# Edges sorted in two halves, the second while the first is written, then added; lists sorted by levels within the rounds

## The reference

```python
# 1: gated graph layer, five rounds on h = layernorm(x)
m = h @ weight[i]
agg = segment_sum(m[src] * edge_attr[:, None], dst)
h = gru_cell(agg, h, w_ih, w_hh, b_ih, b_hh)
# 2: gelu layer with 8 experts, one chosen per node
# 3: graph attention with 8 heads over the same src, dst (sums by src)
# 4: 16 experts, two chosen per node, layernorm
```

## Time and profile before

| | us |
|---|---|
| median of three runs (lowest, highest) | 6021.33 (6021.12, 6024.78) |
| the profiled execution | 6021.4 |
| its span in the trace | 6020.1 |
| PE busy in the span | 4223.5 |
| DVE busy | 2594.2 |
| POOL busy | 2375.9 |
| ACT busy | 1810.6 |

### The profile page before, as it was taken

The page is one execution under the profiler, slowest core; times in us unless marked ns, Lnnn a source line. Parts: engine busy times, 40 slices in busy tenths (PEclk is TensorE's granted clock), DMA queues, the critical chain, the costliest instruction groups (busy, mean ns, idle before and its releaser), DMA issues. The chain is left out here.

```text
span 6020.1 us, 61157 instructions
## 1 busy us (share of the span) xinstructions
PE 4223.5 (70%) x17097; PEld 2593.1 (43%) x17097; DVE 2594.2 (43%) x5613; ACT 1810.6 (30%) x3960; POOL 2375.9 (39%) x2850
## 2 busy tenths in 40 slices
PE   1111113457999999999997859477787767996693
PEld 0110101223544545545444337366666654554372
DVE  8887760112222222122124113655555567776235
ACT  4551000000000101001001311466666648995121
POOL 3336777777000000000000022577777756884303
PEclk9998556778999999999999878799989988997697
DMA  9001001121332231322231323488778855776223
GB/s 397 7 0 46 1 3 44 44 88 44 109 108 98 97 109 65 125 95 86 105 114 43 112 77 117 130 244 242 235 242 242 242 179 171 237 237 226 68 65 111
DMA packets 366136, 752.69 MB, mean 125 GB/s; under 512 B 81332, under 2 KB 186328, under 8 KB 346105
## 3 DMA queue, kind: packets, MB, share of 16 engines
q1 hardware_dynamic: 234825, 575.73, 27.5%
q0 software_dynamic: 77328, 145.78, 9.4%
q10 hardware_dynamic: 53664, 27.26, 1.6%
HBM read 538.83 MB, written 209.74 MB: 124 GB/s over the span
## 5 line engine op out<-in xcount | busy, mean ns | idle before, releaser
L929 PE MATMUL PS<-mem 128*128 128x512 f32 (+1 forms) x3500 | 1363.6, 551 | 318.5 <-DMA mem<-adjacency 314.6
L929 PEld LDWEIGHTS PS<-mem 128*128 128x128 f32 x3500 | 629.5, 192 | 1035.8 <-issue 718.8
L1698 POOL DMA_INDIRECT mem<-gat_rows,mem x832 | 810.4, 974 | 258.2 <-issue 230.0
L522 POOL DMA_INDIRECT adjacency<-mem x782 | 777.3, 994 | 284.1 <-issue 253.4
L1034 DVE COPY mem<-PS 128x512 f32<-128x512 f32 (+1 forms) x35 | 21.8, 624 | 1631.3 <-PE PS L929 1631.3
L1073 POOL MEMSET mem<- 128x256 f32 x1 | 0.3, 311 | 1773.1 <-ACT mem L980 1773.1
L250 PE MATMUL PS<-mem 112*128 112x112 f32 (+3 forms) x462 | 106.5, 410 | 625.6 <-DVE mem L363 272.7
L993 ACT ACTIVATE mem<-PS 128x512 f32<-128x512 f32 (+1 forms) x35 | 19.0, 543 | 1615.6 <-PE PS L929 1615.6
L2042 PE MATMUL PS<-mem 128*128 128x264 f32 x1660 | 451.5, 410 | 29.5 <-DVE mem L2002 19.6
L1733 PE MATMUL PS<-mem 128*128 128x128 f32 x1664 | 280.3, 295 | 248.6 <-DMA mem<-gat_rows,mem 247.9
L1779 ACT ACTIVATE mem<-PS,mem 128x256 f32<-128x256 f32 x832 | 424.4, 561 | 13.7
(11 more groups left out here) (386 smaller groups left out, 6766.0 us busy)
## 6 DMA issues: line engine op xcount, KB each, us to landing
mem<-adjacency SPq DMA_DIRECT2D x150, 1280.0 KB, 5.4
gathered_rows<-mem SPq DMA_DIRECT2D x416, 264.0 KB
mem<-gathered_rows SPq DMA_DIRECT2D x208, 528.0 KB, 4.4
adjacency<-mem SPq DMA_DIRECT2D x56, 800.0 KB, 20.7
mem<-edge_slots ACTq DMA_DIRECT2D x26, 1024.0 KB, 8.3
mem<-w SPq DMA_DIRECT2D x32, 512.0 KB
mem<-gat_rows,mem POOLq DMA_INDIRECT x832
hidden_rows<-mem SPq DMA_DIRECT2D x25, 512.0 KB, 3.0
```

The source lines that it names most:

```text
L522: g.indirect_dma_start(AD[:, :], bass.IndirectOffsetOnAxis(ap=aidx[:, k:k + 1], axis=0), SF[:, k:k + 1], None).then_inc(s[f"scattered{n % ...
L929: ins = t.matmul(PS[:, f, 0:n], lhsT=h[:, b, f * 128:(f + 1) * 128], rhs=m.pan[i % NPAN][:, j, 0:n], start=(b == 0), stop=(b == NB - 1))
L1698: g.indirect_dma_start(m.Dg[i % RING][:, k, j, :], None, HD[:, :], bass.IndirectOffsetOnAxis(ap=L.idxD[:, c:c + 1], axis=0)).then_inc(s[f" ...
```

## The change

The edges are taken in two halves of 50,000, in the order in which they come (so the second has no smaller `dst` than the first). Each half is sorted on 98x512 values (four turns' worth of 128 columns instead of seven; 392 values on the N side) with 136 steps and 18 turns, and has its own key, weight, sum and address buffers. The first half goes as before. Its 391 scatters then run on POOL while DVE, ACT and PE sort the second half; since POOL is taken, DVE makes the masks of the second half itself, with a third compare per step. When all scatters of the first half have landed, POOL issues those of the second with `compute_op=ALU.add`, so that a cell which both halves hold gets both sums; the region behind the matrix is zeroed too. The counts for the panels are those of the second half.

The list sort is cut into levels. The first steps and levels 1 to 3 come before the rounds; levels 4 to 10 and the last part come one each after an iteration q of the rounds, levels 4 to 8 in the first round at q = 0 to 4, the rest in the second at q = 0 to 2. Each level has a turn at the start of PE's next q and one after the third panel of its gather, both in one PSUM bank, so that the second four transposes wait until DVE has read the first four. For this the turned h uses one bank instead of two. There are three panel buffers instead of four, loads for lists and rounds are issued right after the zeroing instead of after the edge sort, and the lists are stored behind the last panel.

```diff
-T1 = 784
+HALF = E // 2
+ROWS1 = 98
+T1 = 4 * ROWS1
...
+    if second:
+        masks, _ = like(m.D[n % NK], old)
+        if n >= NK:
+            v.wait_ge(*s["swapped"](n - NK + 1))
+        for (a, b), k in zip(old, masks):
+            ins = v.tensor_tensor(k, a, b, ALU.is_gt)
+        ins.then_inc(s["mask"].sem, 1)
...
-NCELL = (E + 127) // 128
+NCELL = (HALF + 127) // 128
 CGRP = 8
...
+            g.wait_ge(*sc[f"{name}{n % 2}"](16 * CGRP * (n // 2)))
+        at = bass.IndirectOffsetOnAxis(ap=aidx[:, k:k + 1], axis=0)
+        if add:
+            g.indirect_dma_start(AD[:, :], at, SF[:, k:k + 1], None,
+                                 compute_op=ALU.add).then_inc(sc[f"{name}{n % 2}"].sem, 16)
+        else:
+            g.indirect_dma_start(AD[:, :], at, SF[:, k:k + 1], None).then_inc(sc[f"{name}{n % 2}"].sem, 16)
...
+def listed_at(l, q):
+
+    if q < 5:
+        level = EARLY + 1 + 5 * l + q
+        return level if level <= LAST_LEVEL + 1 else None
...
+def lists_turn(t, m, s, PS, ident, turn, banks):
+
+    level, back = turn // 2 + 1, turn % 2
+    i, n, _ = steps_until(level)
+    if back:
+        i, n = i + level + 1, n + level
+    t.wait_ge(*s["keys"](n))
+    parts = list(turn_parts(m, "toT" if back else "toN", m.K[i % 2], 0))
+    for h in range(2):
+        t.wait_ge(*s["turned"](1 + 2 * turn + (h if banks[0] == banks[1] else 0)))
+        for src, (_, rows, cols) in parts[4 * h:4 * h + 4]:
+            ins = into(t, PS, (src, (banks[h], rows, cols)), ident)
+        ins.then_inc(s["kt"].sem, 1)
...
-NPAN = 4
+NPAN = 3
...
         for q in range(NG + 1):
+            level = listed_at(l, q - 1) if q else None
+            if level:
+                lists_turn(t, lm, li, PS, ident, 2 * level - 2, BANKS)
             if q < NG:
-                rounds_gather(t, m, s, PS, l, q)
+                rounds_gather(t, m, s, PS, l, q, ident, lm, li, level)
...
+        if k == 2 and level and level <= LAST_LEVEL:
+            lists_turn(t, lm, li, PS, ident, 2 * level - 1, BANKS)
...
-    t.wait_ge(*s["ht"](NB + i - 1))
+    t.wait_ge(*s["ht"](NB + i))
...
+            level = listed_at(l, q)
+            if level and level <= LAST_LEVEL:
+                lists_level(v, lm, cn, li, PS, level, BANKS)
+            elif level:
+                lists_last(v, lm, L, li, lst, PS, BANKS)
```

More of the change, by code:

```diff
@@ L154, in network @@
             yield "T", "plain", 1 << i
-    for level in range(1, 11):
+    for level in range(1, levels + 1):
         yield "toN", level, 0
@@ L373, in edges_swap @@
     new, _ = halves(m.W[where][1 - buf][0:P], C, kind, block)
-    masks, mask = like(PS[:, 4 + n % NMASK, :].bitcast(I32), old)
+    masks, mask = like((m.D[n % NK] if second else PS[:, 4 + n % NMASK, :]).bitcast(I32), old)
     v.wait_ge(*s["mask"](n + 1))
@@ L405, in edges_vector @@
                 v.wait_ge(*hd["table"](16))
-            edges_order(v, m, cn, s, PS, plan, i)
+            edges_order(v, m, cn, s, PS, plan, i, second)
         if i >= 2 and plan[i - 2][0] in "TN":
-            edges_swap(v, m, s, PS, *plan[i - 2])
-CELLS = "step edges_ps nb_rows nb_ps local tails_ps carry carry_ps sums back sf cells scattered0 scattered1 held held_ps due"
-def cells_memory(ar, ed, cn):
-    m = Box()
[L419 to L424, removed]
-    return m
+            edges_swap(v, m, s, PS, second, *plan[i - 2])
@@ new lines, with cells_memory @@
+CELLS = {"edges_ps": 1, "nb_rows": 2, "nb_ps": 1, "local": 2, "tails_ps": 1, "carry": 1, "carry_ps": 1, "sums": 2, "back": 1,
+         "sf": 1, "cells": 1}
+SCATTER = "step first0 first1 scattered0 scattered1 held held_ps due"
+def cells_memory(ar):
+    m = Box()
+    m.EQ, m.SX = ar.mk(513)[0:ROWS1], ar.mk(512)[0:ROWS1]
+    m.rows = ar.mk(6, ROWS1)
+    m.cinc, m.aone = ar.mk(1)[0:ROWS1], ar.mk(1)[0:ROWS1]
+    m.ki, m.ia, m.ib = (ar.mk(512, dt=I32)[0:ROWS1] for _ in range(3))
+    m.fa = ar.mk(512)[0:ROWS1]
+    return m
@@ L627, in lists_tensor, with lists_first @@
              stop=True).then_inc(s["counts_ps"].sem, 1)
[L628 to L648 removed]
+    for turn in range(2 * EARLY):
+        lists_turn(t, m, s, PS, cn.ident, turn, EARLY_BANKS)
+def lists_first(v, m, cn, s, st, PS):
     A, K = m.A, m.K
@@ new lines, in lists_level0, with lists_level @@
+def lists_level0(v, m, s):
+    i = 0
+    for k in range(1, 8):
+        for e in range(k, 0, -1):
+            lists_compare(v, m, s, i, i, 0, "T", "flip" if e == k else "plain", 1 << e)
+            i += 1
+def lists_level(v, m, cn, s, PS, level, banks):
+    i, n, turn = steps_until(level)
+    for where, steps in (("toN", level), ("toT", 7)):
+        for h in range(2):
+            v.wait_ge(*s["kt"](2 * turn + h + 1))
+            turn_keys(v, m, cn, PS, where, level, m.K[(i + 1) % 2], banks[h], h).then_inc(s["turned"].sem, 1)
+        i, turn = i + 1, turn + 1
+        for e in range(steps, 0, -1):
+            kind = "flip" if where == "toN" and e == level else "plain"
+            lists_compare(v, m, s, i, n, 2 * turn, where[2], kind, 1 << e)
+            i, n = i + 1, n + 1
```

447 lines of the change are left out of this document (235 added, 212 removed).

## The result

The changed kernel takes 6153.5 us (median of 4 runs, 6152.67 to 6155.08), the kernel before beside it 6023.06 (6021.12 to 6028.02): **1.0216 times as long, 95% interval 1.0198 to 1.0233**. I had forecast 5929 us. The profiled execution took 6153.57 us with a span of 6152.3, 132.2 us more than the span of before.

A forecast was written before the change was run, and what follows sets the result against it. GpSimd's back-to-back scatters bound the start, until q=5; TensorE bound the rounds after. 6020.1 - 121.8 (q=5 earlier) + 29.8 (list turns) = 5928 us span, so 5929 us; range 5850 to 6230.

The forecast's parts named there:

- The path: Before the rounds fill TensorE: edge sort, then GpSimd's scatters back to back, then q=5 and everything after; list sort off it.
- r = 1.45: Second half on GpSimd: us per accumulating scatter, between 1.27 and 2.20; q=5 starts at 1389, 121.8 us earlier; chance 0.37.
- rival B: GpSimd's accumulating scatter: the read side pays twice, 2.20 us each, 6222 us; deciding from 1.69; mild loss up to it 0.17.
- A: GpSimd's second half: accumulating is as cheap as plain, 1.28 us a scatter, q=5 188 us earlier, 5863 us; chance 0.26.
- C: GpSimd's accumulating scatter: a slow path building lists row by row, 4.07 us each, 6951 us; chance 0.15.
- D: Change fails to do what it says: first half starts late or second sort not ready at 815; about 6020 us; chance 0.05.
- the first scatter: After the shorter edge sort, ending at 277 us: 290 us (275 to 315) instead of 480.
- The first half: 391 scatters on GpSimd beside a sorting VectorE: 391 x 1.335 = 522 us, then 3 us wait; second half starts at 815.
- the wait between the halves: On GpSimd, until all scatters of the first half have landed: a new wait of 3 us.
- the second sort hidden: Second half's sort on VectorE and ScalarE beside the first half's scatters: ready at 580, cover 235 us, costed at nothing.
- the lists: List turns inside the rounds on TensorE: 2.8 us in q=5's gather, the rest in round 2; 29.8 us in all.
- The three panel buffers and the single bank: Panel loads and h turns in the rounds: three buffers for four and one bank cost nothing.

The follow-up runs named there:

- e5: The changed kernel again, only loading the registers with the panels' scatter counts one at a time, with bounds; 6156.42 us against 6026.4, ratio 1.0214.
- e8: The kernel of e6 with the second sort's masks written to PSUM instead of SBUF; 5860.51 us, ratio 0.9722.
- e7: The changed kernel with every other scatter of the second half plain instead of accumulating; one run, 6046.97 us, 109 less than e5.
- e6: The changed kernel with only the second half's first 8 scatters accumulating and the list sort ahead of the rounds; 5905.39 us against 6026.4, ratio 0.9794.
- e1: The changed kernel with all 391 scatters of the second half plain; 6443.98 us against 6547.79 on a slower chip, ratio 0.9841.
- e2: The kernel before with all its 782 scatters accumulating; 6717.35 us against 6547.79 on a slower chip, ratio 1.026.
- e11: The changed kernel, second half's scatters alternating plain and accumulating, with 128 and 64 rows; one run, 6259.17 us beside 6557.87 on a slower chip.
- e10: The changed kernel, second sort's mask copied to PSUM by ScalarE and read there by the predicated copies; 6419.13 us beside 6557.87 on a slower chip.
- e9: The changed kernel without the second sort's predicated copies, its three compares a step staying in SBUF; 6413.15 us beside 6557.87 on a slower chip.
- e3: The changed kernel with the whole list sort ahead of the rounds, second half still accumulating; 6366.76 us against 6547.79 on a slower chip, ratio 0.9725.
- e4: The changed kernel with the second sort's masks written to PSUM instead of SBUF; 6412.89 us against 6547.79 on a slower chip, ratio 0.9795.

## Why the prediction was wrong

**The path was right.** Edge sort, POOL's scatters, q=5. On the chip of e5 to e8 the end moved with q=5: e7 is 109.5 us shorter than e5 with q=5 111.6 earlier, e8 45 shorter than e6 with q=5 41.6 earlier, and e6 251 shorter than e5 with q=5 224.6 earlier and 27.6 of list turns gone. On the two slower chips this does not hold (e1, e2).

**The step that failed is the price of the accumulating scatter, r = 1.45.** It is 1.886 us (1.552 + 0.30 and a few longer ones). Of the 217.3 us between the forecast start of q=5 (1389) and the real one (1606.3) this is 390 x 0.436 = 170. It lies beyond 1.69, the point from which I had said that rival B's side decides; with r = 1.886 and everything else as forecast the sum would have been 6099 us, slower than before. That the 6153.5 us lie below the 6230 that I had given as the upper end is no merit of the working. The argument behind 1.45 was that a fixed part rules, so that a second read costs a fifth of a gather. e11 confirms the premise and refutes the conclusion: 64 rows fewer save 0.06 us, but the accumulation brings a fixed part of its own, by my estimate some 0.42 us (0.60 - 2 x 0.09). Between bounds of 1.27 and 2.20 I took a value near the lower one on an argument; the rows bore out neither end.

**Rival B was right in sign and place, wrong in mechanism and size.** The extra is 0.594 us, not a whole second list of 0.946. The Trainium skill (GPSIMD Engine Reference, "4. When to use GPSIMD") says that one core of a pair emits the read descriptors and the other the write descriptors; no run here shows the two cores, and the price does not double. **A** and **C** are refuted by the duration of 1.552 us and the landing of 3.1 (e7), **D** by the first scatter at 271.8 and the second half's sums at 532.9.

**The first half, 525 us forecast, took 586.6.** 38.5 of it are the one scatter held by DVE, 22 the distance of the others (1.392 for 1.335), 1 the handover. I had taken DVE's hold on POOL from the list sort, whose compares have both operands in SBUF, and not asked what the predicated copy does once its mask moves from PSUM to SBUF. e8 gets 45 us of this back, from the long scatter and from the distance beside the sort. The Trainium skill (SBUF — State Buffer, "Who interferes with whom") says that only operations of DVE in a two-port mode, or with two SBUF inputs against a GpSimd operation that reads SBUF, shut GpSimd out, and for the length of an instruction. The trace agrees that DVE can hold GpSimd, and in e10, where the predicated copy reads one operand fewer from SBUF, nothing is held. It differs on the length: compares with two SBUF inputs do not hold a scatter beyond 1.8 us (e9), and with predicated copies whose mask, source and target all lie in SBUF one scatter is held for 39.4 us, through 24 steps and the compares between, while later ones beside the same steps take about 1 us; the measurement decides.

**Right:** the first scatter but for a size (290 forecast, 271.8, just below the lower bound of 275; the sort ended at 255.5 instead of 277), the wait between the halves (3 forecast, 4.4), the second sort hidden by 325 us, and the lists: 29.8 us forecast, 3.2 + 27.5 = 30.7 measured, with e3 and e6 showing the 27.5 gone. The three panel buffers and the single bank cost nothing: with them in place e3's second round is 416.3 us long. For the list store this is not shown. Of the 5.6 us that remain 5.4 lie behind the last gather product, near which the store now stands, and no run tells it from the stages there.

The parts add up: -18.2 + 61.6 + 170 + 4.3 (q=5 follows the last scatter's start by 12.4 us, not 8.1) = 217.7 us at q=5, and 5929 + 217.7 + 0.9 (lists) + 5.6 = 6153 us.

## What to carry to other kernels

When an engine's instruction is the pace, a new mode of that instruction is the first thing to measure, before anything is built around it: here 0.594 us times 391, 232 us, outweighed halves that are 121 us faster than the kernel before when all but eight scatters are plain (e6, which also has the lists ahead of the rounds). If parts can overlap only in a few places, let only those accumulate. And when operands move from PSUM to SBUF, look in the trace whether an engine that runs beside them is held: here it cost one scatter 39 us, and keeping the mask in PSUM gave 45 us back.

## What the runs showed of the hardware

An accumulating transfer of 128 single values moves 144 packets where a plain one moves 32: 43,792 packets more in q0's total (121,120 for 77,328), over 391 scatters, 112 each; in e2 it is 87,584 more over 782, again 112 each. In 900 to 1500 us the queue's row reads

```profile
q0 software_dynamic: 46311, 0.19, 21.4%
```

where the kernel before had 1.8% of the sixteen DMA engines' time in its scatters. At 21% this was no bound: the accumulating scatters of e7 landed in 3.1 us at the median.

On the two chips where the kernel before takes 6548 and 6558 us, PE, and DVE too, go through stretches in which they wait for their own issue. The timeline of PE in e1:

```profile
1184.43 1.01 PE L1024 MATMUL PS<-mem 128*128 128x512 f32 x1 [2.22 <-issue]
1187.21 1.01 PE L1024 MATMUL PS<-mem 128*128 128x512 f32 x1 [1.77 <-issue]
```

One product in 2.8 us, where the kernel after, as first measured, has 26 of them in 11.3 us. In e1 and e4 such stretches begin while POOL issues plain scatters; the 832 gathers behind the rounds are spaced at 1.53 us in e1 and 1.28 in the kernel after, with the same median duration of 0.95. That these two chips deliver instructions late beside POOL's transfers would fit all of it, but no run tells that apart from other causes. It stays open.
